# Feed-forward groups: a third bank for up products, down products three groups behind, copies of y four groups behind

## The chip, the cores and the metric

One core of a Trainium2 chip runs the kernel. The metric is the device time in microseconds (us) of one execution; lower is better. The kernel before was run three times: 1350.55, 1354.19 and 1358.74 us, median 1354.19.

## The reference

The input is 32 x 256 tokens of 128 features (8192 tokens). A mixture-of-experts feed-forward is added, then attention, then the same feed-forward again.

```python
def _L0_ffn_ref(x, gate_w, expert_bias, w1, w2):          # 8 experts with weights, 4 "zero" experts, top 2
    logits = jnp.einsum('btd,ed->bte', x, gate_w) + expert_bias
    topk_logits, topk_idx = jax.lax.top_k(logits, TOP_K)
    topk_w = jax.nn.softmax(topk_logits, axis=-1)
    ...
    h = jax.nn.silu(jnp.einsum('btd,efd->btef', x, w1))    # 128 -> 256 per expert
    y = jnp.einsum('btef,edf->bted', h, w2)                # 256 -> 128
    return jnp.einsum('bte,bted->btd', w_ffn, y) + w_zero[..., None] * x

x = x + 0.5 * _L0_ffn_ref(_layernorm(x), ...)
x = x + _L0_attn_ref(_layernorm(x), ...)                   # 16 heads of 8, a prior added to the scores, softmax
x = x + 0.5 * _L0_ffn_ref(_layernorm(x), ...)
```

## The kernel before, in words

The engines' programs are written out by hand, each as one list of instructions in order, with semaphores between them. The names below are those of the code.

*Expert phases.* The 64 tiles of 128 tokens are cut into segments, `SEG`: ten of them, 0 to 4 for the first feed-forward, 5 to 9 for the second. Segments 0, 1, 8 and 9 have 8 tiles, the others 16. For each segment the tokens are routed (norm, gate logits, two choices, a slot for each copy of a token), scattered by GpSimd's indirect DMAs (L924) into rows sorted by expert, and then worked on in groups of 256 rows, each of one expert: 15 groups for 8 tiles, 23 for 16, 198 in all. `experts(q, nxt)` on each engine is one phase. Phases 0 and 1 come first, one after the other; phases 2 to 7 stand between turns of attention (`PHASES`: in front of batches 4, 7, 12, 18, 25, 29); phases 8 and 9 come last.

*One group n.* SyncE loads its columns (`x_cols`, L334, a ring of six). TensorE makes the up product (`up`, L472 to L474, six matmuls of 256 columns, high and low bf16 parts) into a bank of `U`. ScalarE takes silu twice from that bank: `h_f` in fp32 (L776, a ring of three) and `h_hi` in bf16 (L778, a ring of four). VectorE makes `h_lo` (L1223, `low_part`). TensorE makes the down product (`down`, L487 to L490, twelve matmuls) into a bank of `Y`, two banks, in turn. ScalarE copies it to `y_rows` (L784, `take_y`), SyncE stores that (L343), and later GpSimd gathers the rows back (L938) and VectorE combines them.

*The order.* In iteration g TensorE issues up g and then down g-2; ScalarE silu g and then the copy of y g-2; VectorE the low part of g. Up n waits for silu n-2 (`hi_ready`), silu n for low part n-3 and for down n-4, down n for low part n and for copy n-2 (`y_ready`).

*What stands between.* `plan(nxt)` hangs the routing of the next segment on the iterations, after each engine's own work for the group: token norms on VectorE at 3, 4, 6, 7, transposes (L422) at 5, 6, 8, 9 and gate logits (L431) at 6, 7, 9, 10 on TensorE, the two choices on VectorE at 11 and 12, the count of ranks on TensorE at 14, bases and slots on VectorE at 15 and 16 (for 16 tiles). In phase 1 the first attention batch is prepared too: its norm on GpSimd, transposes on TensorE at 12 (`turn_tokens_of`, L544) and q and k at 14 (`project`), with ScalarE's `token_cols_of` (L821) and `high_part` (L828) in the same iterations, and VectorE's `token_low` (L1356) at 13 and `low_part_of` (L1362) at 15.

*GpSimd in a phase.* `beside_block` spreads gathers or scatters over the groups: each waits for a count of `y_ready` (phases 1 and 3 to 7) or `hi_ready`. The roots of the next segment's norms (`token_root`, L899 and L902) and, in phase 1, the first attention norm (`batch_norm`, L970 to L983) stand between them in the same queue. SyncE stores the y of group g-9 behind the load for group g.

*Banks.* PSUM has eight banks. In a phase 0 and 1 are `U`, 2 and 3 `Y`, 4 gate logits and ranks (`GR`), 7 the transposed tokens (`TF`). In attention 6 and 7 are `M`. `banks_left` and `banks_back` wait, between a turn and a phase, until the one's banks are free for the other.

## Time and profile before

| | |
|---|---|
| runs | 1350.55, 1354.19, 1358.74 us |
| profiled execution, first to last instruction (span) | 1338.4 us; the page gives no other time of it |
| mean granted TensorE clock over the span | 0.896 |
| TensorE busy / VectorE busy / ScalarE busy / GpSimd busy | 1003.1 / 906.0 / 716.5 / 621.8 us |
| instructions | 37494 |
| ten expert phases, first up product to last copy of y | 465.0 us |

The profile is of one execution. In its rows PE is TensorE, PEld its weight loads, DVE VectorE, ACT ScalarE, POOL GpSimd, SP SyncE; Lnnn is a line of the kernel. A row of a timeline has its start in us from the span's start, its duration, engine, line, operation and the tiles that it writes and reads; in brackets the idle time of the engine before it and what ended it ("remote" is a signal whose sender the profile doesn't tell, "issue" no wait that it shows). A row of the waits has who waited for whom, the us in total, how many times, and the longest. A row of the stretches has from and to, its length, the busy us of PE, PEld, DVE, ACT and POOL with the number of instructions, the granted TensorE clock (1 is full), the busy share of the DMA engines and GB/s. A matmul's duration overlaps that of the next.

### The profile page before, as it was taken

To read this page: it belongs to the slowest core of one execution; us is meant where nothing else is said; L and a number is where in the kernel's file an instruction comes from. 1 tells how busy PE (TensorE), PEld (TensorE's weight loads), DVE (VectorE), ACT (ScalarE), POOL (GpSimd) and SP (SyncE) were. 2 spreads that over 40 slices of the span, in tenths; PEclk is the share of its full clock that TensorE was granted. 3 is DMA by queue.
4 is the path that set the end of the run, shared out by engine and by line. 5 is a ranking of instruction groups with operands and counts; after the bars stand their busy time and mean duration, and the time that the engine had idled before them with its cause. 6 is when DMAs were issued, how large, how long until landed. Compare 5 with 4: busy or idle time off the path is not lost.

```text
span 1338.4 us, 37494 instructions
## 1 busy us (share of the span) xinstructions
PE 1003.1 (75%) x13558; PEld 656.9 (49%) x13558; DVE 906.0 (68%) x2405; ACT 716.5 (54%) x1486; POOL 621.8 (46%) x697
## 2 busy tenths in 40 slices
PE   1468587788778888888888888898888876774770
PEld 1346243475447544574444754454754465433560
DVE  4548776685566787866887758877867853654524
ACT  1157344567355755667556575555675555442650
POOL 2556256404544544354542544544445445543554
PEclk9989699998788999998999889988999987785886
DMA  8354535352135311362112731123621274130464
GB/s 247 78 125 107 152 98 173 70 131 55 58 68 131 84 52 60 82 149 60 48 58 65 141 87 53 47 61 73 137 81 53 62 162 113 48 90 19 110 145 113
DMA packets 248881, 125.30 MB, mean 94 GB/s; under 512 B 124384, under 2 KB 238925, under 8 KB 248448
## 3 DMA queue, kind: packets, MB, share of 16 engines
q1 hardware_dynamic: 232320, 94.01, 27.2%
q0 software_dynamic: 16384, 28.89, 8.9%
q8 instruction: 116, 1.90, 0.6%
q14 instruction: 61, 0.50, 0.1%
HBM read 36.25 MB, written 65.31 MB: 76 GB/s over the span
## 4 chain that ended last, share of the span: by engine, by line
PE 39%; DVE 27%; issue 15%; ACT 8%; another core or an unknown queue 7%; POOL 2%; DMA 1%; SPq 1%; DVEq 0%; POOLq 0%; ACTq 0%
PE banks L594 10%; DVE row_max L1329 9%; PE banks L623 4%; PE banks L569 3%; ACT probs L849 3%; DVE h_lo L1223 3%; PE banks L561 2%; PE banks L474 2%; ACT h_hi L778 2%; PE banks L431 2%; PE banks L472 2%; PE banks L487 2%; PE banks L490 2%; DVE stats L1094 2%
## 5 line engine op out<-in xcount | busy, mean ns | idle before, releaser
L849 ACT ACTIVATE probs<-banks 128x512 f32<-128x512 f32 x512 | 280.1, 595 | 313.0 <-PE banks L594 270.4
L1329 DVE TENSOR_REDUCE row_max<-banks 128x2 f32<-128x512 f32 x512 | 330.9, 685 | 100.5 <-PE banks L594 65.2
L938 POOL DMA_INDIRECT big<-yg,slots x256 | 255.2, 997 | 278.3 <-ACT y_rows L784 84.0
L924 POOL DMA_INDIRECT xg<-xs,slots x256 | 253.6, 991 | 274.7 <-PE banks L594 167.8
L1223 DVE TENSOR_TENSOR h_lo<-h_f,h_hi 128x512 bf16<-128x512 f32 x198 | 134.5, 688 | 156.7 <-ACT h_hi L778 118.5
L623 PE MATMUL banks<-probs,v_op 128*32 128x256 f32 x2048 | 202.2, 413 | 10.7 <-ACT ot_sb L842 3.0
L569 PE MATMUL banks<-q_op,k_op 32*128 32x256 bf16 x1024 | 152.2, 293 | 64.7 <-issue 46.0
L594 PE MATMUL banks<-band_parts,thirds 96*32 96x296 bf16 (+2 forms) x4096 | 189.7, 294 | 1.3 <-issue 1.3
L487 PE MATMUL banks<-w_all,h_hi 128*128 x792 | 157.6, 229 | 43.1 <-DVE h_lo L1223 21.6
L561 PE MATMUL banks<-k_op,q_in 32*128 32x256 bf16 x1024 | 154.7, 295 | 37.8 <-DVE row_max L1329 31.5
L776 ACT ACTIVATE h_f<-banks 128x512 f32<-128x512 f32 x198 | 119.8, 605 | 114.3 <-PE banks L474 71.5
L472 PE MATMUL banks<-x_cols,w_all 128*128 128x256 bf16 x396 | 116.5, 294 | 52.2 <-ACT h_hi L778 15.5
L490 PE MATMUL banks<-w_all,h_lo 128*128 x792 | 153.3, 228 | 1.9 <-issue 1.9
L489 PE MATMUL banks<-w_all,h_hi 128*128 x792 | 154.0, 229 | 1.1 <-issue 1.0
L594 PEld LDWEIGHTS banks<-band_parts,thirds 96*32 96x32 bf16 x4096 | 103.4, 100 | 67.0 <-issue 66.6
L778 ACT ACTIVATE h_hi<-banks 128x512 bf16<-128x512 f32 x198 | 120.0, 606 | 0.0
L569 PEld LDWEIGHTS banks<-q_op,k_op 32*128 32x128 bf16 x1024 | 50.6, 93 | 137.2 <-issue 107.4
L474 PE MATMUL banks<-x_cols,w_all 128*128 128x256 bf16 x396 | 116.3, 294 | 1.1 <-issue 1.1
L473 PE MATMUL banks<-x_cols,w_all 128*128 128x256 bf16 x396 | 116.6, 294 | 0.0
L784 ACT ACTIVATE y_rows<-banks 128x256 f32<-128x256 f32 x198 | 77.7, 395 | 67.0 <-PE banks L490 35.0
L487 PEld LDWEIGHTS banks<-w_all,h_hi 128*128 128x128 bf16 x792 | 81.1, 102 | 62.4 <-issue 57.8
L623 PEld LDWEIGHTS banks<-probs,v_op 128*32 128x32 f32 x2048 | 83.5, 117 | 26.9 <-issue 19.6
(173 smaller groups left out, 1668.6 us busy)
## 6 DMA issues: line engine op xcount, KB each, us to landing
yg<-y_rows SPq DMA_DIRECT2D x198, 128.0 KB
k_op<-kq_kept SPq DMA_DIRECT2D x96, 64.0 KB
q_in<-kq_kept SPq DMA_DIRECT2D x96, 64.0 KB
xg<-zeros SPq DMA_DIRECT2D x2, 2944.0 KB
xg<-xs,slots POOLq DMA_INDIRECT x256
big<-yg,slots POOLq DMA_INDIRECT x256
kq_kept<-kq_hi SPq DMA_DIRECT2D x32, 128.0 KB
kq_kept<-kq_lo SPq DMA_DIRECT2D x32, 128.0 KB
```

The source lines that it names most:

```text
L487: pe.matmul(o, h_hi[:, n % 4, cols], w_hi, start=c == 0 and j == 0, stop=False, skip_group_check=True)
L489: pe.matmul(o, h_hi[:, n % 4, cols], w_lo, start=False, stop=False, skip_group_check=True)
L490: mm = pe.matmul(o, h_lo[:, n % 4, cols], w_hi, start=False, stop=c == 1, skip_group_check=True)
L561: return pe.matmul(banks[:, MX[v % 2], bass.ts(k, L)], q_in[r:r + 32, par, g, bass.ts(qt, P)], k_op[r:r + 32, par, g, :], start=k == 0, st ...
L569: return pe.matmul(banks[:, ST[(16 * b + u) % 3], bass.ts(k, L)], k_op[r:r + 32, par, g, bass.ts(kt, P)], q_op[r:r + 32, g, :], start=k == ...
L594: return pe.matmul(banks[32 * r:32 * r + 32, bank, :].rearrange("p (k c) -> p k c", k=2)[:, :, c0:c1], thirds[:], bc(band_parts[:, first:f ...
L623: mm = pe.matmul(banks[32 * j:32 * j + 32, PV, bass.ts(k, L)], v_op[:, par, kt, J * (2 * gp + k) + j, :], probs[:, w // 2 % 2, j, bass.ts( ...
L849: act.activation(probs[:, q % 2, u % 4, :], banks[:, ST[(16 * b + u) % 3], :], ACT.Exp).then_inc(A["exp_done"], 1)
L924: pool.indirect_dma_start(xg[q], bass.IndirectOffsetOnAxis(slots[:, q % 4, c, t:t + 1], 0), xs[:, q % 2, t, :], None, bounds_check=groups[ ...
L938: pool.indirect_dma_start(y_back[:, i, c, :], None, yg[q], bass.IndirectOffsetOnAxis(slots[:, q % 4, c, t:t + 1], 0)).then_inc(gathered[i] ...
L1223: dve.tensor_tensor(h_lo[:, n % 4, :], h_f[:, n % 3, :], h_hi[:, n % 4, :], ALU.subtract).then_inc(C["lo_ready"], 1)
L1329: dve.tensor_reduce(row_max[:, gp, :, qt, j], banks[:, MX[v % 2], :].rearrange("p (k c) -> p k c", k=2), AX.X, ALU.max).then_inc(A["max_do ...
```

## The change

Three things. The up products use three banks in turn, 0, 1 and 6; up n waits for silu n-3. In iteration g TensorE issues down g-3 after up g, and ScalarE copies y g-4 after silu g; both loops run over so many iterations more. Bank 6 is in use by attention's batch 0 in phase 1, so that batch (and it alone) takes bank 7 for its transposes and its q and k, and TensorE waits for them to be read (`kq_ready`) before the first turn of attention. `Y` keeps two banks, the rings of `h_f`, `h_hi`, `h_lo`, `x_cols` and `y_rows` keep their lengths, and VectorE's order, GpSimd's and SyncE's are as before.

```diff
--- before.py
+++ after.py
@@ -407,9 +407,14 @@
             sp.wait_ge(out_stored, 16 * (NSEG - HALF))
 
 
-        U, Y, GR, TF = (0, 1), (2, 3), 4, 7
+        U, Y, GR, TF = (0, 1, 6), (2, 3), 4, 7
         ST, MX, PV, M = (0, 1, 4), (2, 3), 5, (6, 7)
         RK = 256
+        BEHIND = 3
+
+        def cols_bank(b):
+
+            return M[0] if b else M[1]
 
         @block.tensor
         def _(pe):
@@ -463,10 +468,10 @@
             def up(q, g, e):
                 n = G0[q] + g
                 pe.wait_ge(cols_in[n % RX], 16 * (n // RX + 1))
-                wait(pe, C["hi_ready"], n - 1)
+                wait(pe, C["hi_ready"], n - 2)
                 hi, lo = x_cols[:, n % RX, 0, :], x_cols[:, n % RX, 1, :]
                 for c in range(2):
-                    o = banks[:, U[n % 2], bass.ts(c, GS)]
+                    o = banks[:, U[n % 3], bass.ts(c, GS)]
                     w_hi = w_all[:, bass.ds(e + c * P, P)]
                     w_lo = w_all[:, bass.ds(e + 256 + c * P, P)]
                     pe.matmul(o, w_hi, hi, start=True, stop=False)
@@ -495,15 +500,15 @@
                 ng = groups[q]
                 at = plan(nxt)
                 pe.wait_ge(R["owners_ready"], q + 1)
-                for g in range(ng + 2):
+                for g in range(ng + BEHIND):
                     if g == 0:
                         held.update(zip(range(8), load_owners(q, 0)))
                     if g < ng:
                         up(q, g, held[g])
                     if g % 8 == 7 and g + 1 < ng:
                         held.update(zip(range(g + 1, g + 9), load_owners(q, g + 1)))
-                    if 2 <= g < ng + 2:
-                        down(q, g - 2, held.pop(g - 2))
+                    if g >= BEHIND:
+                        down(q, g - BEHIND, held.pop(g - BEHIND))
                     for what, i in at.get(g, ()):
                         if what == "turn":
                             turn_tokens(nxt, i)
@@ -526,6 +531,8 @@
 
             def banks_back(q, nxt=None):
 
+                if q == 1:
+                    pe.wait_ge(A["kq_ready"], 1)
                 pe.wait_ge(C["hi_ready"], G0[q + 1])
                 pe.wait_ge(C["y_ready"], G0[q + 1])
                 if nxt:
@@ -541,14 +548,14 @@
                 wait(pe, A["kq_ready"], b)
                 wait(pe, A["x_added"], b - 3)
                 for t in range(KT):
-                    mm = pe.transpose(banks[:, M[0], bass.ts(t, P)], a_xn[:, t, :], ident_f[:])
+                    mm = pe.transpose(banks[:, cols_bank(b), bass.ts(t, P)], a_xn[:, t, :], ident_f[:])
                 mm.then_inc(A["xn_turned"], 1)
 
             def project(b):
 
                 wait(pe, A["xt_ready"], b + 1)
                 for which, w_hi, w_lo in ((0, wq_hi, wq_lo), (1, wk_hi, wk_lo)):
-                    o = banks[:, M[0], bass.ts(which, L)]
+                    o = banks[:, cols_bank(b), bass.ts(which, L)]
                     pe.matmul(o, w_hi[:], a_xt_hi[:], start=True, stop=False)
                     pe.matmul(o, w_hi[:], a_xt_lo[:], start=False, stop=False)
                     mm = pe.matmul(o, w_lo[:], a_xt_hi[:], start=False, stop=True)
@@ -773,9 +780,9 @@
                 n = G0[q] + g
                 wait(act, C["up_done"], n + 1)
                 wait(act, C["lo_ready"], n - 2)
-                act.activation(h_f[:, n % 3, :], banks[:, U[n % 2], :], ACT.Silu)
+                act.activation(h_f[:, n % 3, :], banks[:, U[n % 3], :], ACT.Silu)
                 wait(act, C["down_done"], n - 3)
-                act.activation(h_hi[:, n % 4, :], banks[:, U[n % 2], :], ACT.Silu).then_inc(C["hi_ready"], 1)
+                act.activation(h_hi[:, n % 4, :], banks[:, U[n % 3], :], ACT.Silu).then_inc(C["hi_ready"], 1)
 
             def take_y(q, g):
                 n = G0[q] + g
@@ -787,14 +794,14 @@
             def experts(q, nxt=None, zero=()):
                 ng = groups[q]
                 at = plan(nxt)
-                for g in range(ng + 2):
+                for g in range(ng + BEHIND + 1):
                     if g < ng:
                         silu(q, g)
                     if 4 <= g:
                         for i in zero[g - 4:g - 3]:
                             add_zero_expert(*i)
-                    if 2 <= g < ng + 2:
-                        take_y(q, g - 2)
+                    if g > BEHIND:
+                        take_y(q, g - BEHIND - 1)
                     for what, i in at.get(g, ()):
                         if what == "turn":
                             token_cols(nxt, i)
@@ -818,14 +825,14 @@
 
                 wait(act, A["xn_turned"], b + 1)
                 wait(act, A["v_done"], b)
-                act.activation(a_xt_hi[:], banks[:, M[0], 0:L], ACT.Copy).then_inc(A["xt_hi_ready"], 1)
+                act.activation(a_xt_hi[:], banks[:, cols_bank(b), 0:L], ACT.Copy).then_inc(A["xt_hi_ready"], 1)
 
             def high_part(b):
 
                 wait(act, A["kq_done"], b + 1)
                 wait(act, kq_out, 32 * b)
                 for which in range(2):
-                    i = act.activation(kq_hi[:, which, :], banks[:, M[0], bass.ts(which, L)], ACT.Identity,
+                    i = act.activation(kq_hi[:, which, :], banks[:, cols_bank(b), bass.ts(which, L)], ACT.Identity,
                                        bias=bias_col[:, which:which + 1])
                 i.then_inc(A["kq_hi_ready"], 1)
 
@@ -1353,13 +1360,13 @@
             def token_low(b):
 
                 wait(dve, A["xt_hi_ready"], b + 1)
-                dve.tensor_tensor(a_xt_lo[:], banks[:, M[0], 0:L], a_xt_hi[:], ALU.subtract).then_inc(A["xt_ready"], 1)
+                dve.tensor_tensor(a_xt_lo[:], banks[:, cols_bank(b), 0:L], a_xt_hi[:], ALU.subtract).then_inc(A["xt_ready"], 1)
 
             def low_part_of(b):
 
                 wait(dve, A["kq_hi_ready"], b + 1)
                 for which in range(2):
-                    i = dve.scalar_tensor_tensor(kq_lo[:, which, :], banks[:, M[0], bass.ts(which, L)],
+                    i = dve.scalar_tensor_tensor(kq_lo[:, which, :], banks[:, cols_bank(b), bass.ts(which, L)],
                                                  bias_col[:, which:which + 1], kq_hi[:, which, :], ALU.add, ALU.subtract)
                 i.then_inc(A["kq_ready"], 1)
```

## Rows read from the trace of the kernel before

**Rows 1.** The page: busy time of each engine, share of the span, instructions.
```profile
PE 1003.1 (75%) x13558; PEld 656.9 (49%) x13558; DVE 906.0 (68%) x2405; ACT 716.5 (54%) x1486; POOL 621.8 (46%) x697
```

**Rows 2.** Stretches: phase 8, and the sum of all ten phases.
```profile
1234.50:1273.00 38.50, 27.47 (x270) 22.18 (x270) 20.99 (x58) 23.06 (x53) 20.55 (x21) 0.83 0.42 108
...
sum 465.00, PE 366.45 PEld 310.95 DVE 295.37 ACT 294.53 POOL 217.38; mean PE 36.64 PEld 31.10 DVE 29.54 ACT 29.45 POOL 21.74
```

**Rows 3.** Waits of the whole run, total us, times, longest.
```profile
DVE h_lo L1223 <- ACT h_hi L778: 118.5, 73, 5.8
...
ACT y_rows L784 <- PE banks L490: 35.0, 50, 2.5
...
ACT y_rows L784 <- remote: 26.9, 14, 4.3
...
PE banks L487 <- DVE h_lo L1223: 21.6, 26, 3.0
...
ACT h_f L776 <- remote: 21.2, 7, 6.2
...
PE banks L472 <- ACT h_hi L778: 15.5, 10, 5.6
...
PE banks L487 <- ACT y_rows L784: 13.4, 8, 3.1
```

**Rows 4.** Timeline of VectorE, then TensorE, first part of phase 2.
```profile
277.59 1.11 DVE L1109 TENSOR_SCALAR xn<-x_all,meanvar,rstd 128x128 f32<-128x128 f32 x4
...
282.28 0.69 DVE L1223 TENSOR_TENSOR h_lo<-h_f,h_hi 128x512 bf16<-128x512 f32 x1 [1.12 <-ACT h_hi L778]
...
279.05 0.61 PE L422 MATMUL banks<-ident_f,xn 128*128 128x128 f32 x4
```

**Rows 5.** Timeline of TensorE, then ScalarE, last eight groups of phase 2.
```profile
297.32 0.27 PE L472 MATMUL banks<-x_cols,w_all 128*128 128x256 bf16 x1
...
297.98 0.22 PE L487 MATMUL banks<-w_all,h_hi 128*128 x1
...
298.65 0.27 PE L472 MATMUL banks<-x_cols,w_all 128*128 128x256 bf16 x1
...
301.37 0.38 ACT L784 ACTIVATE y_rows<-banks 128x256 f32<-128x256 f32 x1 [0.78 <-PE banks L490]
...
304.32 0.39 ACT L784 ACTIVATE y_rows<-banks 128x256 f32<-128x256 f32 x1
304.67 0.60 ACT L776 ACTIVATE h_f<-banks 128x512 f32<-128x512 f32 x1
...
305.64 0.39 ACT L784 ACTIVATE y_rows<-banks 128x256 f32<-128x256 f32 x1
```

**Rows 6.** Timeline of TensorE, start of phase 8.
```profile
1245.57 0.39 PE L472 MATMUL banks<-x_cols,w_all 128*128 128x256 bf16 x1 [5.56 <-ACT h_hi L778]
...
1246.82 0.32 PE L487 MATMUL banks<-w_all,h_hi 128*128 x1
...
1248.10 0.42 PE L472 MATMUL banks<-x_cols,w_all 128*128 128x256 bf16 x1
```

**Rows 7.** Timeline of GpSimd, ScalarE, VectorE, second half of phase 1.
```profile
124.87 1.03 POOL L938 DMA_INDIRECT big<-yg,slots  x1 [1.44 <-ACT y_rows L784]
...
126.68 0.61 ACT L776 ACTIVATE h_f<-banks 128x512 f32<-128x512 f32 x1
...
129.26 0.38 ACT L821 ACTIVATE a_xt_hi<-banks 128x256 bf16<-128x256 f32 x1 [1.22 <-PE banks L544]
...
133.69 0.41 DVE L1356 TENSOR_TENSOR a_xt_lo<-banks,a_xt_hi 128x256 bf16<-128x256 f32 x1
```

**Rows 8.** Timeline of GpSimd, ScalarE, start of phase 3.
```profile
397.49 1.65 POOL L902 TENSOR_TENSOR rstd<-var_eps,neg_half 128x8 f32<-128x8 f32 x1
...
397.06 0.60 ACT L776 ACTIVATE h_f<-banks 128x512 f32<-128x512 f32 x1
```

**Rows 9.** What engines waited for before instructions on x_cols: us, times.
```profile
  DMA x_cols<-xg: 4.2, 2
```

## The prediction

> **What bounds the kernel now.** I read the page first, then the ten stretches of feed-forward work one by one, then the waits, then the timeline of one phase. No engine is full: TensorE is busy for 75% of the span, VectorE 68%, ScalarE 54% [rows 1]. The change touches only the ten expert phases. From the first up product to the last copy of y they take 465.0 of the 1338.4 us [rows 2], so nothing here is worth more than a share of a third of the time. A routed phase (23 groups, routing of a later segment beside it) has two parts. In the first, VectorE sets the pace: in the phase that begins at 259.5 the four norms of 277.59 lie amid other work that leaves no hole, and its first wait for a silu after them is one of 1.12 us, before 282.28 [rows 4]; then come the two top choices, for which TensorE waits before it counts the ranks. In the second part, the last eight groups, TensorE and ScalarE go in step, one group each 1.33 us (up product to up product 297.32 to 298.65 [rows 5]).
>
> The waits that the change aims at are small in sum: TensorE in front of a down product for `h_lo` 21.6 us in 26 times, in front of an up product for `h_hi` 15.5 us in 10 times, ScalarE in front of a copy of y for the down product 35.0 us in 50 times. A wait of the same kind points the other way: TensorE waited 13.4 us in 8 times for a copy of y [rows 3].
>
> **The durations.** Up product: six matmuls issued in 0.66 us (297.32 to 297.98), signal 0.82 us after the first begins. Down product: 0.67 us (297.98 to 298.65). Silu pair: 0.97 us from its start to the start of what follows (304.67 to 305.64), `h_hi` ready after 1.09. Copy of y: 0.35 us (304.32 to 304.67) [rows 5]. At half clock the up product takes 1.25 us (1245.57 to 1246.82) and the down product 1.28 (1246.82 to 1248.10) [rows 6].
>
> **The change part by part.** No instruction is added except one wait, none is removed; all is order and one more bank.
>
> *What the third bank lets happen.* Up n waits for silu n-3 in place of n-2. But look at what stands ahead of it in TensorE's queue. Before up n comes down n-4. Down m waits for copy of y m-2, since y still has two banks, so down n-4 waits for copy n-6. ScalarE now issues that copy after silu n-2. So up n still can't begin before silu n-2 has ended, which is what two banks asked for; it now also waits for one copy (0.35) and one down product (0.67). The loop over two groups is silu 0.97, copy 0.38 to its end, down 0.67, up to its signal 0.82, with some 0.02 to 0.05 for each of the hand-overs: 2.9 us, against 2 x 1.33 = 2.66 of today. In the saturated part that is 0.12 us a group, about 1 us for eight groups. On the other side down product g-3 no longer waits for an `h_lo` that VectorE delivers late: in the second part of this phase copy 17 waits 0.78 us for its down product [rows 5]; that goes, and with it TensorE's wait. I set gain and loss against each other here: 0, with -1 to +1.5 us a phase.
>
> *Down products further behind, first part.* At group 9 TensorE runs down 7 ahead of the last token transposes (they start at 279.05), whose input VectorE's four norms from 277.59 have ready at 278.70 [rows 4]. With the change down 6 stands there and is long done; transposes, gate logits and up 10 come 279.05 - 278.70 = 0.35 us earlier, at most by the whole down product, 0.67. That shortens VectorE's wait of 1.12. Six phases route 16 tiles beside them: 6 x -0.35 = -2.1 us. Bounds -0.67 x 6 = -4 and 0.
>
> *Copies of y further behind.* In phase 0 two copies fewer stand ahead of the last silu, on which, through `h_lo`, VectorE's attention constants and then phase 1 hang: -2 x 0.35 = -0.7 us (bounds -1.3, with one up product at half clock gained at the phase's start, and 0). At the end of each phase four copies are left after the last silu in place of two, and each of the last downs waits for a copy: silu 22 ends, copies 18 and 19, down 21, copy 20, down 22, copy 22. This costs up to 2 x 0.35 = 0.7; it is inside the 0 above. In the last phase, where the gathers of the output stand behind the last copy, nothing sets it off: I take +1.0 us (bounds -0.5 and +2). Phase 8: 0 (the same, bounds -1.3, one up product at half clock that now runs during the stall at its start [rows 6], and +1).
>
> *Who else waits for a copy of y.* GpSimd's gathers are paced by it, and norms stand behind them in its queue. In phase 1 the gather that waits for copy 8 (idle 1.44 us for it, start 124.87) has attention's first norm behind it, and TensorE's transposes of that and group 13's up product stand behind this: ScalarE waited 1.22 us for them at 129.26 [rows 7]. With the copy four groups behind, copy 8 comes after silu 12, which starts at 126.68, so from 127.65 to 128.03; the gather saw it by 124.87: some 3.2 to 3.4 us later. VectorE doesn't take the result before 133.69 because its choices are in front, so most is covered: 129.26 + 3.4 = 132.7 is still earlier. What isn't covered is group 13: its up product stands behind those transposes, at 132.5 its signal comes 0.82 later, silu is done at 134.4, and VectorE's low part of that group stands right ahead of what starts at 133.69, so it would have begun at 133.0: 1.4 us late. One of its own low parts and silus may be earlier by then, so I take +1.0 us (bounds 0 and +3.4). In the routed phases the second half's root (`var_eps`) stands behind the gathers that wait for copy 0. There GpSimd is busy with the first root until 399.14, and copy 0, now behind silu 4 (start 397.06), is there by 397.06 + 0.97 + 0.38 = 398.4 [rows 8]: covered by 0.7 us, so 0; if it weren't, up to +0.7 in each of five phases. SyncE issues the store of a group's y behind the load for nine groups on, and a store two groups later holds back the next load. TensorE waited for such a load 4.2 us in 2 times in the whole run [rows 9], and a load now has six groups of 1.33 us and more: minus two, still 5 us: 0, at most those 4.2 again.
>
> *The other bank for batch 0, the added wait for `kq_ready`.* The wait in front of the first attention turn asks for the low part of batch 0's q and k; the scores behind it need the DMAs of that same result, so only the product for V comes ahead of it today: 0, at most one of VectorE's low parts, +0.7 (0.69 by [rows 4]).
>
> *Sum*: -2.1 + 0 - 0.7 + 1.0 + 1.0 + 0 = -0.8 us on a span of 1338.4, so 1337.6. The page gives no time of the profiled execution beyond its span; the three runs have their median 15.8 us above it, and that I carry over: 1353.4, so 1353 us.
>
> **A rule weighed.** Phase 8 runs at a mean granted clock of 0.83 [rows 2], which is a third of it at the lower level (1.2 in place of 2.4 GHz); after an idle of 5.56 us the up product took 1.25 us where 0.66 is the full rate [rows 5, 6]. The Trainium skill (TensorE: Matmul & The Clock Gate, "HAM oscillation") names exactly small idles between groups that cycle through PSUM banks as what makes the clock swing, which would speak for a deeper queue; the same section tells of a kernel where double-buffering PSUM gave no further gain. By the first, the change would win as rival B says; by the second, nothing. The clock of phase 8 agrees that it swings; no row of before can tell which of the two holds for a third bank.
>
> **The rivals.**
> A, slower: *two y banks hold TensorE on a short line.* Where the signals of TensorE's products reach ScalarE late (copy of y 26.9 us in 14 times, silu 21.2 us in 7 times, released by nothing that the profile names [rows 3]) TensorE comes back at half clock. Today the next up product needs one silu only. With the change it stands behind copy and down product: 1.25 + 1.28 = 2.5 us against ScalarE's 1.3 for silu and copy, so 1.2 us lost each time. 21 such times: 25 us at most; about half are in the parts where VectorE is the bound or at a phase's start, where no copy is asked for yet. +12: 1366 us. It decides from six uncovered losses on (7 us). For it: the order of the waits in the code, and the 13.4 us in 8 times. Against: ScalarE then no longer waits for down products (35.0 us).
> B, faster: *the slack is real.* If the waits for `h_lo` and `h_hi` (21.6 + 15.5) mostly go and ScalarE's 35.0 for down products shrink, a third of the 72 us may come back, half of it already hidden: -12, so 1342 us. For it: VectorE idles in front of `h_lo` 118.5 us for ScalarE [rows 3]. Against: the loop above.
> C, no change in effect: the third bank is never used ahead of its time, and only the orders move. It has the forecast's terms without the -2.1 and the +1.0 of phase 1: about 1354.
>
> **How the numbers follow.** Forecast and C together 0.40, B 0.34, A 0.26. What a measurement of this kernel can tell from no change is about 0.5%, 6.8 us; the three runs alone lie 8 us apart. Faster 0.34, same 0.40, slower 0.26. The bounds above add up to -13 and +24 if every one falls on the same side; they won't, so for the forecast's own range I take a good half below and less than half above, 1345 to 1363; with A and B 1340 to 1366.
>
> **What would show it.** In the trace after: the wait TensorE down <- `h_lo` near zero and TensorE down <- copy of y grown from 13.4 to 30 us or more (if it stays small, the loop argument is wrong and B gains); TensorE's up <- `h_hi` gone; ScalarE copy <- down near zero, and silu <- up grown. The last eight groups of a phase at 1.4 to 1.5 us each in place of 1.33. Phase 1 longer, with the gather's wait for the copy above 1.44 us. The mean clock in phases 7 to 9 lower by A, higher by B.

## The result: 1% slower, outside the range

The changed kernel takes 1372.86 us (median of four runs, 1365.52 to 1374.41); the kernel before, beside it on the same chip, 1354.61 (1350.55 to 1358.74). The ratio is 1.011, interval 1.0067 to 1.0154: 18 us slower. Forecast were 1353 us and 1340 to 1366. Repeated on another chip the ratio is 1.0119 (1.0079 to 1.0159).

That other chip is one of three on which the kernel before takes 1208 to 1211 us; on two it takes 1355 and 1357, as in the first measurement. Ratios below are always against the kernel before on the same chip; "the quicker chips" are the three, "the first chip" is that of the first measurement.

### The profile page after: what moved, and what is told of

The parts are those of the page before. It is cut to its first block, busy times and chain, and to the rows that moved or that the text cites. A ratio compares the mean times of both kernels' runs of the same rounds, so it can differ in the third digit from the quotient of the medians.

```text
span 1371.9 us, 37494 instructions
## 1 busy us (share of the span) xinstructions
PE 1014.6 (74%) x13558; PEld 657.4 (48%) x13558; DVE 905.4 (66%) x2405; ACT 714.4 (52%) x1486; POOL 619.3 (45%) x697
## 4 chain that ended last, share of the span: by engine, by line
PE 44%; DVE 23%; issue 15%; ACT 8%; another core or an unknown queue 6%; POOL 2%; DMA 1%; SPq 0%; DVEq 0%; ACTq 0%; POOLq 0%
PE banks L601 10%; DVE row_max L1336 9%; PE banks L630 4%; PE banks L479 4%; PE banks L576 3%; PE banks L492 3%; PE banks L477 3%; PE banks L494 3%; ACT h_hi L785 2%; PE banks L478 2%; ACT probs L856 2%; PE banks L436 2%; PE banks L568 2%; PE banks L495 2%
## 5 line engine op out<-in xcount | busy, mean ns | idle before, releaser
L945 POOL DMA_INDIRECT big<-yg,slots x256 | 252.5, 986 | 312.3 <-ACT y_rows L791 110.1
L492 PE MATMUL banks<-w_all,h_hi 128*128 x792 | 159.7, 229 | 65.5 <-ACT y_rows L791 44.1
L783 ACT ACTIVATE h_f<-banks 128x512 f32<-128x512 f32 x198 | 119.1, 601 | 160.0 <-PE banks L479 128.5
L477 PE MATMUL banks<-x_cols,w_all 128*128 128x256 bf16 x396 | 120.7, 305 | 40.8 <-issue 13.7
L492 PEld LDWEIGHTS banks<-w_all,h_hi 128*128 128x128 bf16 x792 | 81.4, 103 | 93.9 <-issue 90.8
L479 PE MATMUL banks<-x_cols,w_all 128*128 128x256 bf16 x396 | 120.5, 304 | 2.7 <-issue 2.7
L478 PE MATMUL banks<-x_cols,w_all 128*128 128x256 bf16 x396 | 120.8, 305 | 0.5 <-issue 0.5
L785 ACT ACTIVATE h_hi<-banks 128x512 bf16<-128x512 f32 x198 | 118.8, 600 | 0.0
L791 ACT ACTIVATE y_rows<-banks 128x256 f32<-128x256 f32 x198 | 77.0, 396 | 37.0 <-PE banks L495 20.7
```

Of the source, the lines that this page charges most:

```text
L479: mm = pe.matmul(o, w_lo, hi, start=False, stop=True)
L492: pe.matmul(o, h_hi[:, n % 4, cols], w_hi, start=c == 0 and j == 0, stop=False, skip_group_check=True)
L945: pool.indirect_dma_start(y_back[:, i, c, :], None, yg[q], bass.IndirectOffsetOnAxis(slots[:, q % 4, c, t:t + 1], 0)).then_inc(gathered[i] ...
```

## The profile after

The head of the page and its row of busy times, to be read against [rows 1]:

```profile
span 1371.9 us, 37494 instructions
...
PE 1014.6 (74%) x13558; PEld 657.4 (48%) x13558; DVE 905.4 (66%) x2405; ACT 714.4 (52%) x1486; POOL 619.3 (45%) x697
```

Not one instruction more, and nobody works longer except TensorE (11.5 us more, at a mean clock of 0.891 against 0.896). So nearly all the time is in waits. This execution took 1373.68 us, its span and 1.8 us. By that the profiled execution of before took about 1340, 14 us less than the median; the 33.5 us between the two spans therefore overstate the loss. For sizes I use a pair profiled on one of the quicker chips: spans 1210.2 and 1222.5 (12.3 apart), medians 1208.56 and 1223.01 (14.5 apart). Each run has one trace, and executions of one kernel lie up to some 15 us apart, so differences of a few us between two traces are rough.

The stretches of phases 0, 1, 2 and 8, and the sum of all ten (columns as in [rows 2]):

```profile
59.50:96.00 36.50, 28.04 (x270) 22.28 (x270) 14.41 (x21) 23.30 (x53) 19.23 (x18) 0.86 0.50 111
101.30:148.10 46.80, 33.73 (x343) 28.55 (x343) 36.47 (x125) 26.82 (x62) 23.42 (x24) 0.83 0.42 97
269.50:321.60 52.10, 42.25 (x479) 36.48 (x479) 36.91 (x118) 33.32 (x75) 4.01 (x4) 0.93 0.47 114
...
1263.40:1302.20 38.80, 26.63 (x270) 20.36 (x270) 20.82 (x58) 23.12 (x53) 20.35 (x21) 0.90 0.39 104
...
sum 500.20, PE 376.60 PEld 312.68 DVE 301.14 ACT 292.69 POOL 217.24; mean PE 37.66 PEld 31.27 DVE 30.11 ACT 29.27 POOL 21.72
```

465.0 [rows 2] have become 500.2. The busy sums are nearly as they were, but for TensorE's, which is 10.2 us larger: the loss lies inside the ten phases and is mostly idle time. Outside them the time fell from 873.4 to 871.7.

The waits (who waited for whom: us in total, times, longest), against [rows 3]:

```profile
DVE h_lo L1230 <- ACT h_hi L785: 130.5, 82, 4.6
ACT h_f L783 <- PE banks L479: 128.5, 106, 12.1
POOL big L945 <- ACT y_rows L791: 110.1, 58, 3.7
...
PE banks L492 <- ACT y_rows L791: 44.1, 49, 3.6
...
ACT h_f L783 <- remote: 23.3, 7, 4.8
...
ACT y_rows L791 <- PE banks L495: 20.7, 19, 2.6
...
ACT y_rows L791 <- remote: 11.6, 3, 5.4
```

TensorE now stands 44.1 us in 49 times in front of a down product (L492) for a copy of y; it was 13.4 in 8. ScalarE's wait for up products (`h_f` <- L479) grew from 71.5 in 58 times to 128.5 in 106, and that of GpSimd's gathers for copies (`big` <- `y_rows`) from 84.0 in 42 to 110.1 in 58. What the change aimed at did shrink: down product for `h_lo` to 8.4 us (from 21.6), up product for `h_hi` to 5.6 (from 15.5), copy for down product to 20.7 (from 35.0).

*How the two waits make each other.* Last groups of phase 2: first TensorE, of which the rows are the first matmuls of some of the products (L477 up, L492 down), then ScalarE (L783 and L785 silu, L791 copy):

```profile
308.53 0.27 PE L477 MATMUL banks<-x_cols,w_all 128*128 128x256 bf16 x1
...
309.86 0.27 PE L477 MATMUL banks<-x_cols,w_all 128*128 128x256 bf16 x1
...
311.00 0.23 PE L492 MATMUL banks<-w_all,h_hi 128*128 x1 [0.32 <-ACT y_rows L791]
...
311.74 0.27 PE L477 MATMUL banks<-x_cols,w_all 128*128 128x256 bf16 x1
...
313.07 0.27 PE L477 MATMUL banks<-x_cols,w_all 128*128 128x256 bf16 x1
...
314.20 0.23 PE L492 MATMUL banks<-w_all,h_hi 128*128 x1 [0.32 <-ACT y_rows L791]
```

```profile
309.39 0.60 ACT L783 ACTIVATE h_f<-banks 128x512 f32<-128x512 f32 x1 [0.68 <-PE banks L479]
309.88 0.59 ACT L785 ACTIVATE h_hi<-banks 128x512 bf16<-128x512 f32 x1
310.36 0.39 ACT L791 ACTIVATE y_rows<-banks 128x256 f32<-128x256 f32 x1
310.71 0.60 ACT L783 ACTIVATE h_f<-banks 128x512 f32<-128x512 f32 x1
...
312.60 0.60 ACT L783 ACTIVATE h_f<-banks 128x512 f32<-128x512 f32 x1 [0.52 <-PE banks L479]
```

Numbers behind up, silu, copy and down are those of groups. Up 18 starts at 308.53 and its silu at 309.39 (0.86 later). Copy 14 stands behind that silu, at 310.36 (0.97), and lasts until 310.75 (0.39). Down 16 needs the bank that this copy empties; it starts at 311.00 (0.25). Up 20 stands behind it in TensorE's queue and starts at 311.74 (0.74). That is 3.21 us for two groups, and the same again to up 22 at 314.95: 1.6 us a group where it was 1.33 [rows 5]. The odd groups ride in between and add nothing. Both engines have work left and each waits for the other.

*The end of a phase.* Last up product and last copy of phase 2 in the kernel before, then ScalarE's last rows of phase 2 after:

```profile
303.82 0.27 PE L472 MATMUL banks<-x_cols,w_all 128*128 128x256 bf16 x1
...
307.57 0.38 ACT L784 ACTIVATE y_rows<-banks 128x256 f32<-128x256 f32 x1 [0.94 <-PE banks L490]
```

```profile
318.51 0.38 ACT L791 ACTIVATE y_rows<-banks 128x256 f32<-128x256 f32 x1 [1.07 <-PE banks L495]
319.18 0.38 ACT L791 ACTIVATE y_rows<-banks 128x256 f32<-128x256 f32 x1 [0.29 <-PE banks L495]
321.16 0.38 ACT L791 ACTIVATE y_rows<-banks 128x256 f32<-128x256 f32 x1 [1.60 <-DMA yg<-y_rows]
```

From the last up product (314.95) to the last copy's end (321.54) it is 6.6 us where before it was 4.1. The last copies and downs 20 to 22 alternate; the last copy then waits for the store of copy 18, four places back in the ring `y_rows`. In this trace that wait stands at the end of phases 0 and 2 only, 3.4 us together.

## The experiments

There were two theories to begin with. **Y**: two y banks with copies four groups behind make the loop just read. **L** (rival A as predicted): what costs is TensorE's late signals on the long line. The letters in the expectations are their own: B there blames or credits the third bank itself, D blames the later down products and copies and the longer end of each phase. The first four expectations are in us of the first chip; these runs fell on a quicker one, so they are read by their ratios.

**Which part.** *e1_bank_alone*: three up banks, order of before.

```diff
-        BEHIND = 3
+        BEHIND = 2
-                for g in range(ng + BEHIND + 1):        # ScalarE's loop
+                for g in range(ng + BEHIND):
-                    if g > BEHIND:
-                        take_y(q, g - BEHIND - 1)
+                    if g >= BEHIND:
+                        take_y(q, g - BEHIND)
```

> The third bank for up products alone: down products two groups behind, copies of y two groups behind, as in the kernel before. Theory Y (what costs is that the copy of y m-2, for which down product m waits, now stands behind silu m+2, so that TensorE and ScalarE wait for each other; the third bank has no part in it): the wait of down products for a copy is back at 10 to 20 us, the ten phases at 455 to 470 us, time 1344 to 1357 us. Rival B (the third bank itself, or bank 6 in its double use, costs): 1363 to 1375 us, phases at 485 us or more.

Measured 1209.01 us, ratio 0.9995 (0.9973 to 1.0017): no change.

*e2_order_alone*: the changed order with two up banks.

```diff
-        U, Y, GR, TF = (0, 1, 6), (2, 3), 4, 7
+        U, Y, GR, TF = (0, 1), (2, 3), 4, 7
-                wait(pe, C["hi_ready"], n - 2)
+                wait(pe, C["hi_ready"], n - 1)
```

(and `U[n % 2]` for `U[n % 3]`.)

> The orders alone: down products three groups behind, copies four, but two banks for up products (up n waits for silu n-2 again). Theory Y: the down product in front of an up product already waits for that silu and a copy more, so the third bank is worth nothing here: 1368 to 1378 us, as the changed kernel within 0.5%, wait of down products for a copy 35 to 50 us. Rival B: without the third bank no slower than before, 1350 to 1358 us. Third possibility, the bank does cover something of the order's cost: 1380 us or more.

1220.59 us, 1.0077 (1.0047 to 1.0108), a little below the 1.010 to 1.017 expected. The third bank alone is worth nothing; the order alone costs. Its trace has the loop: down products waited for a copy 22.8 us in 49 times (e1: 11.1 in 14), and in the last groups of phase 2 up products stand 1.32 and 1.88 apart in turn, 3.2 for two.

**Which order.** *e3_copy_3*: copies of y three groups behind, downs and banks as changed.

```diff
-                    if g > BEHIND:
-                        take_y(q, g - BEHIND - 1)
+                    if g >= BEHIND:
+                        take_y(q, g - BEHIND)
```

> The changed kernel with copies of y three groups behind in place of four (down products three behind, three banks). Theory Y: down product m needs the copy that now stands behind silu m+1, one group of distance more than in the changed kernel and as much as before: 1343 to 1358 us, wait of down products for a copy under 20 us, last eight groups of a phase back at 1.35 to 1.5 us each. Rival D (down products further behind are what costs, by the longer end of each phase): 1363 to 1373 us.

1209.36 us, 0.9993 (0.9968 to 1.0019).

*e4_bank_to_y*: changed order, third bank to y.

```diff
-        U, Y, GR, TF = (0, 1, 6), (2, 3), 4, 7
+        U, Y, GR, TF = (0, 1), (2, 3, 6), 4, 7
-                wait(pe, C["y_ready"], n - 1)
+                wait(pe, C["y_ready"], n - 2)
```

(and up n waits for silu n-2 again.)

> The orders of the changed kernel (down products three behind, copies four), but the third bank is given to y in place of the up products. Theory Y: down product m now waits for copy m-3, behind silu m+1: the mutual wait is gone, 1345 to 1360 us, wait of down products for a copy under 15 us, though the four copies at each phase's end remain. Rival D, or one in which the copies' lateness costs by what hangs on them (stores, gathers): 1363 to 1375 us.

1207.41 us, 0.9986 (0.9965 to 1.0008). So the loss needs both, copies four behind and two y banks. And D falls: downs three behind alone (e3) cost nothing, and neither do the later copies once y has three banks (e4). The row of the wait, e2, then e3, then e4:

```profile
PE banks L492 <- ACT y_rows L791: 22.8, 49, 1.1
```
```profile
PE banks L492 <- ACT y_rows L791: 6.2, 16, 0.8
```
```profile
PE banks L492 <- ACT y_rows L791: 4.2, 10, 1.5
```

**The pair of before and after again**, since the chips turned out to differ.

> The kernel before once more, for its trace beside those of the experiments on the same chip. On the chip of the first four experiments it took 1210.69 us and not 1354.61, so its phases should be some 415 us and the gaps that end in a late signal of TensorE (48 us in the first trace) nearly gone.

1208.56 us, 0.9998 (0.9967 to 1.0029). The row of the wait:

```profile
PE banks L487 <- ACT y_rows L784: 8.2, 10, 1.4
```

> The changed kernel once more, beside the same chip's runs of the kernel before. Theory Y: ratio 1.006 to 1.013, like the orders alone (1.0077), since the third bank is worth nothing under these orders; its wait of down products for a copy 20 to 45 us. If the late signals of TensorE made a good part of the loss, a chip without them shows less than the 1.011 of the first: 1.005 to 1.009.

1223.01 us, 1.0119 (1.0079 to 1.0159). The wait again, after_again:

```profile
PE banks L492 <- ACT y_rows L791: 20.7, 44, 1.0
```

No copy and no silu waits for "remote" in either trace, and the ratio is that of the first chip. So L isn't what makes the loss: it doesn't need late signals. The parts of the ten phases, added up from the starts of the up products in the traces:

| us, sum of ten phases | before_again | after_again | difference | e6 (below) |
|---|---|---|---|---|
| first four groups | 59.9 | 50.6 | -9.3 | 54.2 |
| middle | 185.1 | 192.1 | +7.0 | 187.3 |
| last eight, up to the last up product | 125.3 | 135.3 | +10.0 | 120.9 |
| from there to the end of the last copy | 46.4 | 58.6 | +12.3 | 54.1 |
| phases together | 416.7 | 436.7 | +20.0 | 416.5 |
| outside the phases | 793.5 | 785.8 | -7.7 | 792.4 |

Of the +20.0, 8.6 are in phase 1 alone (7.8 of them in its last eight groups). Not all of it reaches the run. Phases 0 and 8 are 2.1 and 2.3 us longer, but the next phase begins as before: from the first up product of phase 0 to that of phase 1 it is 35.2 and 35.0 us, from phase 8 to phase 9 33.1 and 32.9. What is lost there comes off the gaps behind them (8.0 to 5.7 us and 5.7 to 3.2), which is 4.8 of the -7.7. Another 2.6 are in the gap before phase 2 (107.8 to 105.2 us); e1, with the order of before, has 105.6 there, so that part isn't the change's.

**The loop itself.** If Y is right, a copy five behind must make the loop span one group in place of two. *e5_copy_5* does that; GpSimd's gathers and scatters are paced by the silus there, since by the waits in its code the kernel would otherwise stand still.

```diff
-                for g in range(ng + BEHIND + 1):
+                for g in range(ng + BEHIND + 2):
-                    if g > BEHIND:
-                        take_y(q, g - BEHIND - 1)
+                    if g > BEHIND + 1:
+                        take_y(q, g - BEHIND - 2)
-            def beside_block(rows, q, t0, t1, block, done="y_ready", ...):
+            def beside_block(rows, q, t0, t1, block, done="hi_ready", ...):
```

> Copies of y five groups behind in place of four, the rest as changed; GpSimd's pacing counts silus in place of copies (else GpSimd, TensorE and ScalarE would wait for each other in phase 1). Theory Y: down g-3 now waits for the copy behind silu g, and that for up g right ahead of it, so TensorE and ScalarE no longer overlap: 0.82 + 0.97 + 0.39 + 0.25 + 0.67 + 0.04 = 3.1 us for each group after the first five, 148 groups, against 2.2 today: +110 to +190 us on the changed kernel. Rival D (only the longer end of each phase costs): one copy more at ten ends, +4 to +10 us.

1507.75 us, 1.2431 (1.2341 to 1.2521). TensorE, then ScalarE, in e5's phase 2:

```profile
346.05 0.27 PE L477 MATMUL banks<-x_cols,w_all 128*128 128x256 bf16 x1
...
348.52 0.23 PE L492 MATMUL banks<-w_all,h_hi 128*128 x1 [1.64 <-ACT y_rows L791]
349.26 0.27 PE L477 MATMUL banks<-x_cols,w_all 128*128 128x256 bf16 x1
```
```profile
346.91 0.60 ACT L783 ACTIVATE h_f<-banks 128x512 f32<-128x512 f32 x1 [1.85 <-PE banks L479]
...
347.88 0.39 ACT L791 ACTIVATE y_rows<-banks 128x256 f32<-128x256 f32 x1
```

0.86 + 0.97 + 0.39 + 0.25 + 0.74 = 3.21 us again, each term the same, now for every single group. Beside the pacing, which costs nothing by itself (e7 below), only the number of groups on the loop was changed, and the pace went from 1.6 to 3.2. The size was expected too small (+110 to +190 over the changed kernel, measured +285). The middle of the phases, where I had taken VectorE as the bound, went from 192.1 to 349.1 us, and the last eight groups from 135.3 to 251.7, which is 3.6 us a group and not 3.2. Its mean granted clock is 0.854, and of its phases' 715.7 us 316 were at the lower level (after_again: 67 of 436.7); the expectation had no term for that.

*e6_copy_first*: all as changed, but ScalarE takes copy g-4 ahead of silu g.

```diff
                 for g in range(ng + BEHIND + 1):
+                    if g > BEHIND:
+                        take_y(q, g - BEHIND - 1)
                     if g < ng:
                         silu(q, g)
...
-                    if g > BEHIND:
-                        take_y(q, g - BEHIND - 1)
```

> The changed kernel with one thing moved: in each group's turn ScalarE copies y g-4 ahead of silu g and not behind it. Distance, banks, ends of the phases and the number of copies left at them stay. Theory Y (the loss is the wait for a copy that stands behind a silu whose up product stands behind the down product that waits): down g-3 now needs silu g-2 only, ratio to before 0.996 to 1.003, wait of down products for a copy under 15 us, last eight groups of a phase at 1.33 us each where nothing else is late. Rival D (copies four groups behind cost as such): 1.008 to 1.013 as the changed kernel.

1211.09 us, 1.0010 (0.9983 to 1.0037): the loss is gone by moving the copy one place in ScalarE's queue, with the same banks and the same down products. Its phase 2, ScalarE, then its wait row:

```profile
281.86 0.60 ACT L783 ACTIVATE h_f<-banks 128x512 f32<-128x512 f32 x1
282.36 0.59 ACT L785 ACTIVATE h_hi<-banks 128x512 bf16<-128x512 f32 x1
282.83 0.39 ACT L791 ACTIVATE y_rows<-banks 128x256 f32<-128x256 f32 x1
283.19 0.60 ACT L783 ACTIVATE h_f<-banks 128x512 f32<-128x512 f32 x1
```
```profile
PE banks L492 <- ACT y_rows L791: 7.0, 17, 1.1
```

A group each 1.33 us, ScalarE without a hole. The last column of the table splits the change: with the loop taken out, the new order gains 5.8 us at the starts and 4.4 in the last eight groups and pays 7.7 at the ends and 2.3 in the middles, together nothing (-0.2). The other 20.2 inside the phases (436.7 against 416.5) go with the loop: 14.4 in the last eight groups, 4.7 in the middles, 4.6 at the ends, less 3.5 at the starts. Some 4 of them are phase 1's (41.2 us in e6, 45.3 in after_again), and not all of those are the loop's (see phase 1 below). In the whole run, as the ratios have it (1.0010 against 1.0119), the loop costs some 13 us; most of the rest comes off the gaps behind phases 0 and 8.

**Phase 1.** *e7_pace_hi*: the changed kernel, the gathers paced by silus (e5's last edit alone).

> The changed kernel with GpSimd's gathers and norms paced by silus (hi_ready) in place of copies. Theory P (the later copies hold back GpSimd and what stands behind in its queue, the first attention norm in phase 1 above all): 2 to 6 us less than the changed kernel, all in phase 1. Theory Y alone: within 2 us of the changed kernel. It also is the base for the run with copies five groups behind.

1221.48 us, 1.0100 (1.0058 to 1.0143). Phase 1 takes 36.7 us in before_again, 45.3 in after_again, 39.1 here. No gather waits for a copy here, and attention's norm comes 25.2 us after the phase's first up product, in after_again 32.3. But some 3 of the 6.2 us between the two traces are not the gather's: from 16 to 23 us into phase 1 TensorE's granted clock was at the lower of its two levels (1.2 in place of 2.4 GHz) in after_again, and its up products 9 to 12 came 3 us late; in e7 and before_again it was at the full one. The stretch 112 to 115 us, after_again, then before_again:

```profile
112.00:115.00 3.00, 3.00 (x22) 2.62 (x23) 2.69 (x8) 1.53 (x4) 0.34 (x1) 0.50 0.34 75
```
```profile
112.00:115.00 3.00, 3.00 (x40) 2.79 (x38) 2.86 (x8) 2.71 (x7) 2.32 (x3) 1.00 0.68 136
```

And the whole run is only 1.5 us quicker, inside the noise of the two and short of the 2 to 6 expected: in these traces the other phases are longer by as much, and the sum of all ten is the same (436.6 and 436.7).

**A better version?** *e8_y3_copy3*: third bank to y, downs and copies both three behind.

```diff
-        U, Y, GR, TF = (0, 1, 6), (2, 3), 4, 7
+        U, Y, GR, TF = (0, 1), (2, 3, 6), 4, 7
-                    if g > BEHIND:
-                        take_y(q, g - BEHIND - 1)
+                    if g >= BEHIND:
+                        take_y(q, g - BEHIND)
```

(waits: up n for silu n-2, down n for copy n-3.)

> The version that the runs so far point to: three banks for y, two for up products, down products and copies three groups behind. Theory Y: no down product waits for a copy (under 6 us), and the phases' ends are as short as with copies three behind: ratio to before 0.993 to 1.000. If the ends cost nothing it is no faster than the third bank given to y with copies four behind (0.9986).

1201.65 us, 0.9936 (0.991 to 0.9963): faster than before on a quicker chip; phases 406.3 us, their last part 47.1 (the profiled execution was the quickest of the twelve, 4.3 us under the median). *e9_33_two_banks* is the same with two y banks, and *e10_y3_copy3_again* is e8 again; both ran on chips of the slower kind.

> Down products and copies three groups behind, but no third bank for anything: two for up products, two for y. It tells what the third bank for y is worth in the last version (0.9936). Theory Y: the order alone frees nothing more and costs nothing, 0.998 to 1.003; if it is below 0.996, the gain of that version is the order's and not the bank's.

1359.6 us, 1.0017 (0.9991 to 1.0043): without the third bank for y the order neither costs nor gains there.

> The version with three banks for y and both lags at three once more, since the first run of it and the run without the third bank fell on chips of different speed (before at 1210.8 and at 1357.4 us). If its gain doesn't hang on the chip: ratio 0.990 to 0.997 wherever it runs. If it is worth something only where TensorE's signals are never late: 0.998 to 1.003 on a chip where the kernel before takes over 1340 us.

1354.53 us, 0.9977 (0.9947 to 1.0007). So e8's gain is shown on one quicker chip only. Whether it is smaller here or hidden in the noise stays open, and the interval overlaps e9's.

## Why the prediction was wrong

**The step that failed** is the end of "What the third bank lets happen": "I set gain and loss against each other here: 0". The mechanism stood there, with its parts in the right order and in the right queues; its size did not. By e6 the gain and the order's own costs do cancel (-0.2 us over ten phases), and then the loop comes on top: some 20 us in the phases of these traces, some 13 of the run.
- *The loop was taken 0.3 us too short.* I had 2.9, with 0.02 to 0.05 for each hand-over. Measured it is 3.21: copy's end to the down product 0.25, silu pair 0.97, copy 0.39, down to up 0.74 (not 0.67), up to silu 0.86 (not 0.82). Against the 2.66 of before the surplus is 0.55 us in two groups, not 0.24: some 2 us in eight groups where I had about 1 (the last eight groups of the ten phases lost 14.4 us against e6). "1.4 to 1.5 us" a group was 1.6.
- *The gain was used twice.* The new order does win at the starts and in the last eight groups, and down products wait little for `h_lo`, as predicted. I set that gain against the loop, but the order's own cost at the ends (7.7 us in e6) had used it up already.
- *It was counted for six phases.* The bounds of -13 and +24 take the "-1 to +1.5 us a phase" six times; the loop runs in the last eight groups of all ten. Ten times would give -17 and +30.

**The end of a phase** was taken at no more than 0.7 us and called inside the 0. In phases 4 and 5 of the quicker chip, where nothing else disturbs, it is 1.2 (4.14 to 5.37); in all ten 12.3 there and 20.8 on the first chip, the largest single part. I had counted the copies, but not the 0.25 us at each hand-over between copies and down products that alternate through two banks, nor the store four places back, which shows at the ends of two phases on the first chip and of three on the other.

**Phase 1** was +1.0 with an upper bound of +3.4; it is +6.4 on the first chip and +8.6 on the other. The mechanism is the one described, the gather behind a late copy, with attention's norm, its transposes and an up product behind that. In the first chip's traces the norm's first step on GpSimd comes 27.8 us after the phase's first up product before and 29.7 after, and ScalarE now waits 4.85 us where it waited 1.22 [rows 7]. Before, then after:

```profile
125.97 0.19 POOL L970 TENSOR_SCALAR a_var_eps<-a_meanvar 128x2 f32<-128x2 f32 x1
```
```profile
131.04 0.54 POOL L977 TENSOR_SCALAR a_var_eps<-a_meanvar 128x2 f32<-128x2 f32 x1
...
134.61 0.38 ACT L828 ACTIVATE a_xt_hi<-banks 128x256 bf16<-128x256 f32 x1 [4.85 <-PE banks L551]
```

I moved copy 8 by two silus at their undisturbed starts (3.4 us). In the two traces of the quicker chip the norm comes 26.0 and 32.3 us after the phase's first up product, 6.3 later, and up product 13, behind the transposes that need it, is 6.6 later. About half of that is the stretch at the lower clock shown with e7, for which the prediction had no term; on the first chip, without such a stretch ahead of the norm, up product 13 is 2.1 later. The wait has a second price that wasn't counted: TensorE stood idle for 4.2 us in front of those transposes, and the up products behind them ran at the lower level of the clock, 0.42 us a matmul in place of 0.27 (first chip, after; in the trace of before phase 1 is at the full level from 6 us on):

```profile
133.88 0.69 PE L551 MATMUL banks<-ident_f,a_xn 128*128 128x128 f32 x2 [4.22 <-POOL a_xn L990]
134.37 0.42 PE L477 MATMUL banks<-x_cols,w_all 128*128 128x256 bf16 x1
```

By e6, without the loop, the phase is 4.5 us longer than before, by e7, with silus as the count, 2.4. What I took as cover, VectorE's choices, covers the norm's reader there but not the up product.

**Smaller steps.** Phase 0 at -0.7: the phase is 4.3 us longer on the first chip and 2.1 on the other, and the start of phase 1, which the term was about, moved by +2.7 and -0.2. Six phases at -0.35 in their first part: from up 7 to up 10 phase 4 of the quicker chip takes 6.60 us before and 6.65 after, nothing to be seen of it. The last phase at +1.0: +3.8 and +0.5. Phase 8 at 0: +0.4 and +2.3. The start of the phases gained more than foreseen, 6.8 us on the first chip and 9.3 on the other. All runs with downs three behind on the quicker chips have it (47.8 to 55.7 us against 59.9, and 59.1 in e1); the likely reason, read from the order and not tested by itself, is that the first down product now stands behind the fourth up product. Copy 0 and SyncE's loads at 0: phases 3 to 7 show no loss at their start. The added wait for `kq_ready` at 0: the gap behind phase 1 is 121.0 and 121.5 us on the first chip, no longer on the other.

**The rivals.** A was right in sign and in its mechanism (TensorE on a line through copy and down product), and in its sign post of 30 us (44.1). Its price was hung on late signals, 21 times 1.2 us; the quicker chip has none and its ratio is the same. The loop runs through every saturated stretch, as the 1.32 and 1.88 in turn show, and not only after a stall. B fell: by e1 the third bank alone gives nothing, and the waits whose end it counted on came back elsewhere.

**The rule weighed.** The granted clock over the span is 0.891 after and 0.896 before; phases 0 and 1 fell from 0.95 and 0.93 to 0.86 and 0.83, and phase 8 rose from 0.83 to 0.90. On the quicker chips e2 has 0.937 and before_again 0.934, and e2 is 0.8% slower all the same; e6 has 0.918 and after_again 0.926, and e6 is the quicker (within the phases 77 us at the lower level against 67): over the whole run the clock isn't the cause, though in phase 1 it has a share. Of the two statements in the Trainium skill (TensorE: Matmul & The Clock Gate) the first, on small idles between groups that cycle through PSUM banks, stands in the section "A second HAM failure mode: psum-queue depth-cycling" and not in "HAM oscillation". The second, that adding PSUM double-buffering gave a kernel no further gain ("HAM oscillation"), agrees with e1, a third bank for up products (0.9995); it doesn't carry over to y's banks, where the third was worth something on one chip (e8, 0.9936).

**The step from span to time.** The 15.8 us between the span and the median weren't a cost around the span: after runs at span + 1.8. That moved no difference, but it hid that the profiled execution of before was some 14 us quicker than the median.

**Open.** Outside the phases the quicker chips take 783 to 789 us in e2 to e5, e7, e8 and after_again, and 792 to 793 in before_again, e1 and e6. The gaps behind phases 0, 1 and 8 explain after_again; what makes the others isn't known. And of the first chip's 20.8 us at the ends of phases, the waits in front of a phase's last copies show 3.4 for the store (none before) and 11.6 for "remote" (4.2 before). The order's 1.2 us at each of ten ends would make 12. That adds up roughly, but no kernel separates late signals from the order there.

## What to carry to other kernels

Before moving a step further behind, walk the ring that closes through both in-order queues, with the hand-overs, and divide by the number of groups that it spans: here 3.21 us over two groups stood against 2.66 and cost some 13 us of 1210, and over one group it made the kernel 24% slower. Give the spare bank to the ring whose release the move delays (y here: 0.9986 in e4), not to the one in front of it (up products: 1.0119). At the end of a phase nothing new comes behind, so a step moved back is paid there in every phase (1.2 us here), unless what follows waits for something else (phases 0 and 8), and again by whoever is paced on its count (phase 1).

## What the runs showed of the hardware

The same kernel before takes 1208 to 1211 us on three chips and 1355 to 1357 in the other measurements, at mean clocks of 0.934 and 0.896 in the two profiled executions. In the slower traces silus and copies wait 32 to 48 us for signals that the profile can't assign ("remote", up to 6.2 us each [rows 3]); in the quicker ones not at all. From the end of ScalarE's copy to the start of the matmul that waits for it it is 0.25 us, in after and in e5 alike.
